# Causal attention: the sums of weights of three head pairs go through DRAM to 128 rows of 16, are inverted and gated there, and come back spread

## The chip, the cores and the metric

The kernel runs on one core of a Trainium2 chip. The metric is the device time of one execution in microseconds (us), as the median of several executions. Before the change it is 975.06 us, the median of 3 runs from 974.35 to 975.89 us. The profile shows one execution with a timestamp for every instruction.

## The reference, cut to what matters

One decoder layer in fp32 on an input of 2 sequences of 1024 tokens with 256 columns: a linear attention, a cross attention, and a feed-forward part that is a causal attention over gated experts. Only the third part is touched here:

```python
gates = sigmoid(x @ w_gate)                       # 8 heads x 8 experts for every token
sel   = argmax(gates, axis=-1)
gm    = one_hot(sel) * gates                      # the best expert's gate, zero for the others
values = einsum('bhne,ehdk,bnd->bhnk', gm, value_experts, x)
attn  = softmax(causal(q @ k.T))                  # 8 heads, 1024 x 1024
out   = einsum('bhij,bhjk->bhik', attn, values)
out   = einsum('bhne,ehkd,bhnk->bhnd', gm, output_experts, out).sum(axis=heads)
```

A row of the softmax is divided by its sum of weights, and the result is multiplied by the gate of the token before it goes to the output experts. Both factors are one number per head and token. The kernel puts them together: `oT * (1 / sum) * gate`.

## The kernel before, in words

The two sequences ("batches", b = 0 and 1) run one after the other through the same stages. The attention stage takes about 251 to 401 us in the first batch and about 725 to 875 us in the second. The sum over the output experts follows it.

**The attention stage.** The 8 heads are taken in order, two heads forming a pair: the even head has partitions 0 to 63, the odd one 64 to 127. Per head TensorE walks over 12 blocks (4 for the first 512 queries, 8 for the second 512; index n from 0 to 11). A block is a transposed score matmul (L1391, L1392, and a mask at L1394), an exponential on ScalarE (ACT, L749), and a matmul with the values (`weigh`, L1355), two blocks behind. The values carry 64 columns of ones for each pair, so the bank that collects the weighted values of a head on its 64 partitions collects the sum of weights on the other 64, the same sum on every one of them.

The exponentials need the maximum of each score row first. So while head h runs, TensorE also computes the plain scores of head h + 1 (`scores`, L1331), and VectorE (DVE) takes their maxima (`maximum`, L968) from three rotating PSUM banks: the fourth tile of a head can only be written when the first maximum has been taken. These 12 score tiles are spread over blocks 3 to 8 of head h (`SCORES_AT`); at block 9 the maxima are transposed and VectorE writes them as a row (`max_row`, L981), which the blocks of head h + 1 need. In even heads TensorE also makes the query and key projections of the next pair (`project`, L1315, after blocks 3, 5, 7 and 10).

**What VectorE does per head, in its order.** The loop `for h in range(1, H3)` runs `split(h)` (L954, L957: the key in two parts), the 12 maxima, and `max_row(h)`. Around `split(h)`, from h = 3 on, it normalises an earlier half of a pair: `PARTS[k]` is 512 columns of a pair (k = 0, 1 are pair 0; 2, 3 pair 1; 4, 5 pair 2; 6, 7, 8 pair 3, whose second half is cut in two). `inverted` (L989) is a reciprocal of `rden`, 128 partitions by 512 columns in two pieces of 256; `weighted` multiplies `rden` by the gates in `gb` (L997) and then `oT` by `rden` (L999). The parts k = 0 to 4 go into heads 3 to 7, and k = 5 comes behind the loop.

**Where the sums and gates come from.** ScalarE copies each finished bank (`evacuate`, L725 to L732): the sum rows into `rden` (64 x 512), the values into `oT`. `gate_rows` lies in DRAM; `spread_gates` (L716) sends the two gate rows of a pair over 64 partitions each into `gb`, on the DMA queue of ScalarE, at block 5 of each odd head.

**Behind the attention.** For the 32 (expert, pair) combinations in the order `SUMMED` (pair 3 comes first at n = 5), VectorE masks `oT` of the pair (L1043) and its rounding remainder (L1046), `masked(n)`, and TensorE adds 24 matmuls (L1418, L1424). The last three parts are normalised between them: `normalise(6)` after `masked(0)`, `normalise(7)` after `masked(1)`, `normalise(8)` after `masked(4)`. The output experts' pieces lie in two slots; the piece of expert 2 is fetched when TensorE has finished n = 5, the last use of expert 0.

**The order of the queues.** Every engine runs its instructions in program order, each behind its semaphore waits. SyncE (SP) issues almost all DMAs, also in order. In the first batch it loads 16 expert pieces, writes their two rounded halves back to DRAM (`halves_kept`, 512 KB each), and these loads and stores last until well into the attention; in the second batch the halves are read back and the attention stage has no such traffic. SP then fetches the masks (`fetch_mask`, L335).

## Time and profile before

| what | value |
|---|---|
| median of 3 runs | 975.06 us (974.35 to 975.89) |
| span of the profiled execution, first to last instruction | 972.8 us |
| median less that span (what lies around it) | 2.3 us |
| TensorE busy | 934.5 us (96%) |
| VectorE busy | 681.6 us (70%) |
| ScalarE busy | 387.8 us (40%) |
| GpSimd busy | 235.9 us (24%) |
| TensorE's granted clock, mean | 0.998 |

The page gives the span of the profiled execution, not a time of its own; the runs without a profile are 2.3 us above that span. Matmuls are pipelined, so that TensorE's busy time holds some waiting. The profile's "chain that ended last" goes back from the last instruction, at each step to what released it. "Idle before" in a row is the time for which the engine stood still just before that instruction, with what ended it.

### The profile page before, as it was taken

The numbers are of one execution on the slowest core, as the hardware profiler recorded it, in microseconds if no ns is written. First come the engines' busy times: TensorE is split into PE (matmuls) and PEld (weight loads), VectorE is DVE, ScalarE is ACT, GpSimd is POOL, SyncE is SP. The second block draws the span as 40 slices with busy tenths as digits, with TensorE's granted clock in tenths as the row PEclk, the third lists the DMA queues.
The fourth block names the chain that finished last, engine by engine and source line by source line (L and its number), as shares of the span: only waits on it lengthen the run. The fifth ranks groups of instructions, "written<-read, shape, count | busy, mean of one in ns | idle before, by whom it ended". The sixth has DMA issues, their size and how long they took to land.

```text
span 972.8 us, 14708 instructions
## 1 busy us (share of the span) xinstructions
PE 934.5 (96%) x5620; PEld 727.5 (75%) x5620; DVE 681.6 (70%) x1054; ACT 387.8 (40%) x672; POOL 235.9 (24%) x253
## 2 busy tenths in 40 slices
PE   6989999999999999999999998999999999999998
PEld 3668778887666655889976786888876656569998
DVE  4757566547557877888868666754674777879787
ACT  4535555030566766301033455720115655751000
POOL 6312322222533322136610042300041101411000
PEclk9999999999999999999999999999999999999999
DMA  7103000523255511256630000022220000123653
GB/s 257 49 18 114 2 1 5 162 101 130 65 155 193 198 40 44 65 173 175 179 124 1 1 2 1 1 94 87 86 84 4 23 23 0 30 70 109 184 180 124
DMA packets 33739, 81.56 MB, mean 84 GB/s; under 512 B 5847, under 2 KB 10551, under 8 KB 33671
## 3 DMA queue, kind: packets, MB, share of 16 engines
q1 hardware_dynamic: 32391, 76.44, 24.8%
q10 hardware_dynamic: 1280, 4.20, 1.6%
q8 instruction: 45, 0.74, 0.3%
q14 instruction: 23, 0.19, 0.1%
HBM read 61.26 MB, written 19.20 MB: 83 GB/s over the span
## 4 chain that ended last, share of the span: by engine, by line
PE 81%; DVE 10%; issue 3%; ACT 3%; DMA 2%; POOL 0%; ACTq 0%; SPq 0%; DVEq 0%; POOLq 0%
PE ps L1097 18%; PE ps L1418 10%; PE ps L1355 9%; PE ps L1424 5%; PE ps L1315 5%; PE ps L1270 5%; PE ps L1105 4%; PE ps L1331 4%; PE ps L1222 3%; DVE region L989 3%; PE ps L1284 3%; PE ps L1391 3%; PE ps L1392 2%; PE ps L1237 2%; PE ps L1139 2%
## 5 line engine op out<-in xcount | busy, mean ns | idle before, releaser
L1355 PE MATMUL ps<-region 128*128 128x512 f32 (+3 forms) x384 | 161.5, 504 | 0.0
L968 DVE TENSOR_REDUCE region<-ps 128x1 f32<-128x512 f32 (+1 forms) x192 | 98.2, 551 | 63.8 <-PE ps L1334 63.8
L749 ACT ACTIVATE region<-ps 128x512 f32<-128x512 f32 x192 | 92.2, 486 | 123.0 <-PE ps L1394 111.3
L1013 DVE COPY_PREDICATED region<-region,ps 128x512 f32<-128x512 uint32 x112 | 82.0, 736 | 72.0 <-PE ps L1097 71.3
L1418 PE MATMUL ps<-expert_hi,kst 128*128 128x256 f32 x512 | 125.1, 283 | 5.3 <-DMA expert_lo<-halves_kept 3.2
L1418 PE MATMUL ps<-expert_lo,kst 128*128 128x256 f32 x512 | 123.4, 280 | 0.0
L1097 PE MATMUL ps<-expert_hi,wide_hi 128*128 128x512 f32 x256 | 102.8, 401 | 0.0
L1418 PEld LDWEIGHTS ps<-expert_hi,kst 128*128 128x128 f32 x512 | 96.4, 188 | 6.6 <-DMA expert_lo<-halves_kept 3.6
L1097 PE MATMUL ps<-expert_hi,wide_lo 128*128 128x512 f32 x256 | 100.3, 392 | 0.0
L1097 PE MATMUL ps<-expert_lo,wide_hi 128*128 128x512 f32 x256 | 99.9, 390 | 0.0
L549 ACT ACTIVATE region<-ps 64x512 f32<-64x512 f32 (+4 forms) x146 | 80.8, 556 | 46.7 <-PE ps L1237 19.5
L1418 PEld LDWEIGHTS ps<-expert_lo,kst 128*128 128x128 f32 x512 | 96.5, 188 | 0.0
L1043 DVE TENSOR_TENSOR kst<-region 128x1024 fp32r<-128x1024 f32 x64 | 78.5, 1226 | 20.5 <-PE ps L1424 20.5
L421 POOL TENSOR_TENSOR qx<-region,qq 64x1024 fp32r<-64x1024 f32 x16 | 41.7, 2606 | 195.9 <-ACT qq L549 195.8
L1391 PE MATMUL ps<-qq,kst 128*128 128x512 f32 x192 | 86.9, 453 | 1.5 <-ACT region L749 1.3
L1331 PE MATMUL ps<-kst,qq 128*128 128x512 f32 (+1 forms) x192 | 79.7, 467 | 4.4 <-DVE region L968 4.4
L1424 PE MATMUL ps<-expert_hi,qq 128*128 128x256 f32 x512 | 72.5, 280 | 0.0
L1355 PEld LDWEIGHTS ps<-region 128*128 128x128 f32 x384 | 64.4, 194 | 6.2
L1392 PE MATMUL ps<-qx,kx 128*128 128x512 f32 x192 | 66.5, 346 | 0.0
L1424 PEld LDWEIGHTS ps<-expert_hi,qq 128*128 128x128 f32 x512 | 65.3, 188 | 0.0
L410 POOL TENSOR_TENSOR expert_lo<-expert,expert_hi 128x1024 fp32r<-128x1024 f32 x16 | 39.0, 2440 | 99.5 <-ACT expert_hi L549 99.5
L907 DVE TENSOR_REDUCE top<-ps 128x8 f32<-128x512 f32 (+1 forms) x64 | 34.2, 577 | 36.0 <-PE ps L1222 36.0
(148 smaller groups left out, 1772.3 us busy)
## 6 DMA issues: line engine op xcount, KB each, us to landing
region<-hot_rows SPq DMA_DIRECT2D x128, 128.0 KB, 3.4
expert_hi<-halves_kept SPq DMA_DIRECT2D x24, 512.0 KB, 3.6
expert_lo<-halves_kept SPq DMA_DIRECT2D x24, 512.0 KB, 5.0
halves_kept<-expert_hi SPq DMA_DIRECT2D x16, 512.0 KB, 5.1
halves_kept<-expert_lo SPq DMA_DIRECT2D x16, 512.0 KB, 5.9
expert<-in_value_experts SPq DMA_DIRECT2D x8, 512.0 KB, 4.2
expert<-in_output_experts SPq DMA_DIRECT2D x8, 512.0 KB, 4.3
gb<-gate_rows ACTq DMA_DIRECT2D x16, 256.0 KB, 3.8
```

The costliest lines, as they stand in the source:

```text
L549: act.activation(dst, src, ACT.Copy).then_inc(sem[name], 1)
L749: act.activation(PT[:, g % RING, lo:CH], ps[:, 4 + g % 2, 0:CH - lo], ACT.Exp).then_inc(sem["pt_ready"], 1)
L968: dve.tensor_reduce(mx[:, i, at_mx:at_mx + 1], ps[:, max_bank(h, m), 0:w], AX.X, ALU.max).then_inc(sem["s_max"], 1)
L1013: dve.copy_predicated(V3_heads[:, t], chosen.unsqueeze(3).broadcast_to([P, PAIRS3, 2, HD3]), ps[:, n % 4, :].rearrange("p (a i k) -> p a i ...
L1043: dve.tensor_tensor(kst[i][:, :], oT[:, p, :], masks[:, n % MASKS, :], ALU.mult).then_inc(sem["mo_hi_ready"], 1)
L1097: last = mm(ps[:, n % 4, :], x[:, i, rows_of], columns(w, i), start=(k == 0), stop=(k == len(parts) - 1))
L1331: last = mm(ps[:, max_bank(h, m), 0:w], qq[i][:, t * P:(t + 1) * P], kst[i][:, c * CH:c * CH + w], start=True, stop=not diagonal)
L1355: mm(ps[:, SUM_BANK[c], lo:CH], V3[:, j, h // 2, h % 2 * HD3:(h % 2 + 2) * HD3], PT[:, g % RING, lo:CH], start=(j == 0), stop=(j == TC * ( ...
L1391: mm(ps[:, bank, 0:w], kst[i][:, key], qq[i][:, query], start=True, stop=False)
L1392: last = mm(ps[:, bank, 0:w], kx[i][:, key], qx[i][:, query], start=False, stop=j < TC * c)
L1418: mm(ps[:, 4 + t // 2, t % 2 * D:(t % 2 + 1) * D], kst[n % 2][:, t * P:(t + 1) * P], w[:, slot, columns], start=(n == 0 and t % 2 == 0 and ...
L1424: return mm(ps[:, 4 + t // 2, t % 2 * D:(t % 2 + 1) * D], qq[n % 2][:, t * P:(t + 1) * P], expert_hi[:, slot, columns], start=False, stop= ...
```

## The change

For pairs 0 to 2, a sum is no longer inverted on 128 partitions by 1024 columns. ScalarE copies only one row of it per head (1 x 512, into row 32 * (h % 4) of `rden`); SP sends the row to DRAM (`den_rows`), and fetches the two rows of a pair as 128 rows of 16 (`den_cols`). VectorE inverts that 128 x 16 tile and multiplies it by the gates, which SP has fetched in the same layout (`gate_cols`). SP writes the result to DRAM (`factor_rows`), waits, and sends it over 64 partitions per head into `gb`. `weighted` then is one multiplication of `oT` by `gb`. The two tiles lie where the gate logits of the stage before were. Pair 3 keeps the old way. Its gates are spread by ScalarE after the last `evacuate` and no longer at block 5 of the last head; the other calls of `spread_gates` are gone. VectorE normalises the parts k = 0 to 3 in heads 4 to 7, and k = 4, 5 behind the loop.

```diff
+    BY_COLUMNS = PAIRS3 - 1
...
+        KN = 2 * S // P
...
+        hg_all = hg.rearrange("p t n -> p (t n)")
+        gate_cols = hg_all[:, 0:BY_COLUMNS * KN].rearrange("p (a k) -> p a k", a=BY_COLUMNS)
+        den_cols = hg_all[:, BY_COLUMNS * KN:(BY_COLUMNS + 2) * KN].rearrange("p (i k) -> p i k", i=2)
...
+        den_row = lambda h: P // 4 * (h % 4)
...
-        ROUND_AT = {(5, 4): 0, (5, 6): 1, (5, 8): 2, (5, 10): 3, (6, 6): 4, (7, 6): 5}
+        ROUND_AT = {(5, 4): 0, (5, 6): 1, (5, 8): 2, (6, 6): 3, (7, 9): 4, (7, 11): 5}
...
+            def columns_of(rows):
+                return rows.rearrange("h (q k) -> (h q) k", k=KN)
+            def keep_den(b, h):
+                until(sp, "o_sb", b, 2 * (h * NC + 1) + 1)
+                r = den_row(h)
+                sp.dma_start(den_rows[b, h:h + 1, :], rden[r:r + 1, :]).then_inc(den_kept, 16)
+            def turn_den(b, p):
+                n = b * BY_COLUMNS + p
+                sp.wait_ge(den_kept, 32 * (n + 1))
+                if n >= 2:
+                    sp.wait_ge(factors_kept, 16 * (n - 1))
+                sp.dma_start(den_cols[:, p % 2, :], columns_of(den_rows[b, 2 * p:2 * p + 2])).then_inc(den_in, 16)
+            def spread_factors(b, p):
+                n = b * BY_COLUMNS + p
+                until(sp, "factors_ready", b, p + 1)
+                sp.dma_start(columns_of(factor_rows[b, 2 * p:2 * p + 2]), den_cols[:, p % 2, :]
+                             ).then_inc(factors_kept, 16)
+                sp.wait_ge(factors_kept, 16 * (n + 1))
+                until(sp, "oT_ready", b, NC * p)
+                for i in range(2):
+                    sp.dma_start(gb[i * HALF:(i + 1) * HALF, :],
+                                 factor_rows[b, 2 * p + i:2 * p + i + 1, :].broadcast_to([HALF, S])
+                                 ).then_inc(gates_in, 16)
+            def turn_gates(b):
+                sp.wait_ge(rows_kept, 32 * (b + 1))
+                until(sp, "val_v", b, TT * (E3 - 1))
+                for p in range(BY_COLUMNS):
+                    sp.dma_start(gate_cols[:, p, :], columns_of(gate_rows[b, 2 * p:2 * p + 2])
+                                 ).then_inc(gate_cols_in, 16)
...
             for q in range(PIECES):
...
+                if q == E3:
+                    turn_gates(0)
+                if q == E3 + 4:
+                    keep_den(0, 0)
+                    keep_den(0, 1)
+                    turn_den(0, 0)
+                if q == E3 + 6:
+                    spread_factors(0, 0)
                 until(sp, "piece_lo", 0, q + 1)
...
-                sp.wait_ge(rows_kept, 32 * (b + 1))
+                if b:
+                    turn_gates(b)
+                for p in range(BY_COLUMNS):
+                    if b + p:
+                        keep_den(b, 2 * p)
+                        keep_den(b, 2 * p + 1)
+                        turn_den(b, p)
+                        spread_factors(b, p)
                 until(sp, "kst_ready", b, 2 * H3)
...
                     until(act, "av_used", b, h * NB + ENDS[c])
-                    if h % 2 == 0 and h:
-                        until(act, "oT_ready", b, (h // 2 - 1) * NC + c + 1)
-                    copy(rden[own:own + HALF, cs], ps[oth:oth + HALF, SUM_BANK[c], :], "o_sb")
+                    if h < 2 * BY_COLUMNS:
+                        r, n = den_row(h), 2 * BY_COLUMNS * b + h - 3
+                        if n > 0:
+                            act.wait_ge(den_kept, 16 * n)
+                        copy(rden[r:r + 1, cs], ps[oth:oth + 1, SUM_BANK[c], :], "o_sb")
+                    else:
+                        act.wait_ge(den_kept, 32 * BY_COLUMNS * (b + 1))
+                        copy(rden[own:own + HALF, cs], ps[oth:oth + HALF, SUM_BANK[c], :], "o_sb")
...
-                        if h % 2 and n == NB // 2 - 1:
-                            spread_gates(h // 2)
...
                 evacuate(H3 - 1, 1)
+                spread_gates()
                 for k in range(len(ROUND_AT), len(PARTS)):
                     rounded(k)
...
+                def factors(p):
+                    n = b * BY_COLUMNS + p
+                    if p == 0:
+                        dve.wait_ge(gate_cols_in, 16 * BY_COLUMNS * (b + 1))
+                    dve.wait_ge(den_in, 16 * (n + 1))
+                    step(dve.reciprocal(den_cols[:, p % 2, :], den_cols[:, p % 2, :]))
+                    dve.tensor_tensor(den_cols[:, p % 2, :], den_cols[:, p % 2, :], gate_cols[:, p, :], ALU.mult
+                                      ).then_inc(sem["factors_ready"], 1)
                 def weighted(k):
...
-                    step(dve.tensor_tensor(rden[:, cs], rden[:, cs], gb[:, cs], ALU.mult))
+                    if p >= BY_COLUMNS:
+                        step(dve.tensor_tensor(rden[:, cs], rden[:, cs], gb[:, cs], ALU.mult))
...
-                    dve.tensor_tensor(oT[:, p, cs], oT[:, p, cs], rden[:, cs], ALU.mult
+                    dve.tensor_tensor(oT[:, p, cs], oT[:, p, cs], (rden if p >= BY_COLUMNS else gb)[:, cs], ALU.mult
...
                 for h in range(1, H3):
-                    if h >= 3:
-                        _, c0, c1 = PARTS[h - 3]
-                        inverted(h - 3, c0, (c0 + c1) // 2)
                     split(h)
-                    if h >= 3:
-                        inverted(h - 3, (c0 + c1) // 2, c1)
-                        weighted(h - 3)
+                    if h >= 4:
+                        weighted(h - 4)
                     for m in range(NB):
                         maximum(h, m)
                     max_row(h)
-                normalise(H3 - 3)
+                    if h % 2 and h >= 3:
+                        factors((h - 3) // 2)
+                for k in range(H3 - 4, 2 * BY_COLUMNS):
+                    weighted(k)
```

## Rows read from the trace of the kernel before

**Rows 1.** The page: span; the chain that ended last, by engine.

```profile
span 972.8 us, 14708 instructions
...
PE 81%; DVE 10%; issue 3%; ACT 3%; DMA 2%; POOL 0%; ACTq 0%; SPq 0%; DVEq 0%; POOLq 0%
```

**Rows 2.** The whole chain in order of time (start us, us, what): the reciprocals in it.

```profile
314.28 1.76 DVE region L989
...
846.65 1.76 DVE region L989
```

**Rows 3.** VectorE's timeline, second batch (start us, us, engine, line, op, out<-in, count): `max_row` of heads 1 to 4.

```profile
744.04 1.21 DVE L981 SCALAR_TENSOR_TENSOR qx<-ps,const 8x1024 fp32r<-8x1024 f32 x1 [0.61 <-PE ps L1342]
...
762.25 1.22 DVE L981 SCALAR_TENSOR_TENSOR qx<-ps,const 8x1024 fp32r<-8x1024 f32 x1 [0.61 <-PE ps L1342]
...
782.80 1.21 DVE L981 SCALAR_TENSOR_TENSOR qx<-ps,const 8x1024 fp32r<-8x1024 f32 x1 [0.61 <-PE ps L1342]
...
801.96 1.22 DVE L981 SCALAR_TENSOR_TENSOR qx<-ps,const 8x1024 fp32r<-8x1024 f32 x1 [0.61 <-PE ps L1342]
```

**Rows 4.** TensorE's timeline: third and fourth score tile of heads 2, 4 and 7.

```profile
752.17 0.42 PE L1331 MATMUL ps<-kst,qq 128*128 128x384 f32 x1
753.26 0.58 PE L1331 MATMUL ps<-kst,qq 128*128 128x512 f32 x1
...
790.94 0.42 PE L1331 MATMUL ps<-kst,qq 128*128 128x384 f32 x1
793.00 0.49 PE L1331 MATMUL ps<-kst,qq 128*128 128x512 f32 x1 [0.63 <-DVE region L968]
...
373.68 0.42 PE L1331 MATMUL ps<-kst,qq 128*128 128x384 f32 x1
376.10 0.50 PE L1331 MATMUL ps<-kst,qq 128*128 128x512 f32 x1 [0.98 <-DVE region L968]
```

**Rows 5.** VectorE's timeline: the body of head 4, second and first batch.

```profile
792.67 3.07 DVE L968 TENSOR_REDUCE region<-ps 128x1 f32<-128x128 f32 x7
...
318.33 3.07 DVE L968 TENSOR_REDUCE region<-ps 128x1 f32<-128x128 f32 x7
```

**Rows 6.** Line L930: reciprocals of 128 x 16 and 128 x 8 (min/median/max in ns).

```profile
L930 DVE RECIPROCAL rc<-ps x32: 197/232/259, 72.8 to 620.3; 128x16 f32<-128x16 f32 x16, 128x8 f32<-128x8 f32 x16
```

**Rows 7.** DMA issues, 330.2 to 334 us: a store with nothing queued ahead (median us to landing).

```profile
halves_kept<-expert_hi SPq DMA_DIRECT2D x1, 512.0 KB, 2.6
```

**Rows 8.** Line L721: the gates' spread to 64 partitions, 16 DMAs.

```profile
DMA to landing us min/median/max: 3.4/3.8/4.7
```

**Rows 9.** SP's timeline and the DMA share by windows (last columns: clock, share, GB/s).

```profile
310.82 0.43 SPq L352 DMA_DIRECT2D halves_kept<-expert_lo  x1
...
314.00:316.00 2.00, 2.00 (x12) 1.29 (x11) 1.97 (x2) 1.98 (x3) 1.22 (x1) 1.00 0.98 399
316.00:318.00 2.00, 2.00 (x12) 1.28 (x10) 1.93 (x3) 1.98 (x5) 1.14 (x1) 1.00 0.05 16
```

**Rows 10.** ScalarE's timeline, last head: the gates' spread, the last evacuation.

```profile
392.47 0.45 ACTq L721 DMA_DIRECT2D gb<-gate_rows  x1
...
401.31 1.21 ACT L549 ACTIVATE region<-ps 64x512 f32<-64x512 f32 x2 [1.08 <-PE ps L1355]
```

**Rows 11.** VectorE's timeline behind the attention, first batch.

```profile
398.82 0.69 DVE L997 TENSOR_TENSOR region<-region,gb 128x512 f32<-128x512 f32 x1
...
415.33 1.23 DVE L1043 TENSOR_TENSOR kst<-region 128x1024 fp32r<-128x1024 f32 x1
```

**Rows 12.** TensorE's timeline, 402 to 430 us: all rows with idle time before them.

```profile
416.61 0.39 PE L1418 MATMUL ps<-expert_hi,kst 128*128 128x256 f32 x1 [1.05 <-DVE kst L1043]
426.72 0.39 PE L1418 MATMUL ps<-expert_hi,kst 128*128 128x256 f32 x1 [1.24 <-DMA expert_lo<-halves_kept]
```

**Rows 13.** The windows at the end of the span (busy PE, PEld, DVE, ACT, POOL; clock; share).

```profile
968.00:970.00 2.00, 1.27 (x11) 1.07 (x10) 1.98 (x3) 0.00 (x0) 0.00 (x0) 1.00 0.59 194
...
972.00:972.80 0.80, 0.00 (x0) 0.00 (x0) 0.00 (x0) 0.00 (x0) 0.00 (x0) 0.93 0.01 1
```

More of the change, by code:

```diff
@@ L177, in decoder_layer @@
         gate_rows = nc.dram_tensor("gate_rows", (B, H3, S), fp32, kind="Internal").ap()
+        den_rows = nc.dram_tensor("den_rows", (B, H3, S), fp32, kind="Internal").ap()
+        factor_rows = nc.dram_tensor("factor_rows", (B, H3, S), fp32, kind="Internal").ap()
         halves_kept = nc.dram_tensor("halves_kept", (2 * E3, 2, P, 4 * D), fp32, kind="Internal").ap()
@@ L197, in decoder_layer @@
             mo_hi_ready=NEP, mo_lo_ready=NEP,
-            x_lo=TT, windows_clear=1, piece_hi=2 * E3, piece_lo=2 * E3, mo_used=NEP, bank_full=TC - 1, out_ready=TC,
+            factors_ready=BY_COLUMNS, x_lo=TT, windows_clear=1, piece_hi=2 * E3, piece_lo=2 * E3, mo_used=NEP, bank_full=TC - 1, out_ready=TC,
         )
@@ L207, in decoder_layer @@
                 "c2k_ps", "c2v_ps", "c2k_sb", "c2v_sb", "dve_step"))
-        rows_kept, gates_in = (ctx.enter_context(nc.semaphore(n)) for n in ("rows_kept", "gates_in"))
+        rows_kept, gates_in, gate_cols_in, den_kept, den_in, factors_kept = (
+            ctx.enter_context(nc.semaphore(n)) for n in (
+                "rows_kept", "gates_in", "gate_cols_in", "den_kept", "den_in", "factors_kept"))
         x_in = [ctx.enter_context(nc.semaphore(f"x_in{i}")) for i in range(TT // 2)]
@@ L714, in rounded, with spread_gates @@
                     copy(o_lo(p)[:, c0:c1], oT[:, p, c0:c1], "o_round")
-                def spread_gates(p):
+                def spread_gates():
+                    p = PAIRS3 - 1
                     act.wait_ge(rows_kept, 32 * (b + 1))
```

## The prediction, made before the changed kernel was run

> **What bounds the kernel now.** I read the page first: in the chain of work that ended last TensorE has 81% of the span and VectorE 10% [rows 1]. So a microsecond taken from VectorE counts only where TensorE stands still for it. The chain in order of time then says where that may be: for pairs 0 to 2 it passes through twelve stretches of reciprocal (L989) and gate product (L997), six in each batch, 21.0 us together, the first and the last of them in [rows 2]. A chain says who released whom, not how long the other engine waited, so I measured the waiting in two more views.
>
> The first is the distance from one `max_row` to the next, a whole head of TensorE's work. From head 1 to head 2 of the second batch, where VectorE has nothing to invert, it is 762.25 - 744.04 = 18.21 us; from head 3 to head 4, with the same TensorE work and one inversion in VectorE's way, 801.96 - 782.80 = 19.16 us [rows 3]. The inversion, 5.2 us of VectorE, costs 0.95 us. The second is where TensorE pays: between the third and the fourth score tile of a head. Without inversion these are 1.09 us apart, with one 2.06 us, in the last head 2.42 us [rows 4]. So 0.97 us are to be had in heads 4 and 6, and 1.33 us in head 7. In heads 3 and 5 the stretch holds two more projections, and the chain goes through TensorE alone there: nothing to be had. All that the removed work costs is thus 2 x 0.97 + 1.33 = 3.3 us a batch, 6.5 us in all.
>
> Behind the attention it is the other way round. There TensorE waits for VectorE before n = 5 (1.05 us), and then for the expert piece that n = 5 frees (1.24 us) [rows 12]. VectorE works from 398.82 us, the gate product of part 6, to the mask of n = 5 at 415.33 us without a pause [rows 11]. Whatever makes that product late makes the whole rest of the batch late.
>
> **The change part by part.**
>
> *Pair 3's gates.* Before, ScalarE issued their spread at 392.47 us, and they were in before part 6 wanted them at 398.82 us [rows 10, 11]. Now the two DMAs stand behind the last `evacuate`, which can start at 401.31 us. The second is issued one issue (0.45 us) behind the first and lands 3.8 us later [rows 8, 10]: 401.31 + 0.45 + 3.8 = 405.56. `weighted(6)` waits for it on VectorE, and queued behind it are `masked(1)` and everything up to n = 5. So that whole row moves by 405.56 - 398.82 = 6.7 us, and n = 5 with it; its cover, the last six blocks of head 7, is gone. TensorE has only n = 0 to do meanwhile. Ends: with the fastest landing (3.4) it is 6.3 us; if the DMA goes only when the two copies of the evacuation (1.21 us) have ended, with the slowest landing (4.7), 8.9 us. I take 6.7, as ScalarE's queue issued at 392.47 us while its engine still had an exponential ahead of the DMA in program order to run. Twice: **+13.4 us** (12.6 to 17.8).
>
> *The round trip in heads 4 and 6.* `weighted(0)` and `weighted(2)` now come right behind `split`, and want factors which VectorE itself makes only at the end of the head before. Second batch, head 4: `max_row` of head 3 ends at 784.01. The small reciprocal is 0.23 us [rows 6], the product no more, with the handovers 0.55: 784.55. The store to DRAM is not in this trace; the nearest row is a store of 512 KB with a free queue, 2.6 us [rows 7], and I take that for 8 KB in 64-byte pieces: 787.15. Then two spreads, 0.5 and 3.8 us [rows 8]: 791.45. One product: the maxima start at 792.2, where before they started at 792.67 [rows 5]. Of the 0.97 us, 0.5 is gained. Ends: a store that costs nothing gains all 0.97; one of 3.4 us with a spread of 4.7 loses 1.2. The same holds for head 6 of both batches: three times, **-1.5 us** (-2.9 to +3.7).
>
> The Trainium skill ("DMA: Bandwidth & Descriptors", section "Anatomy of one DMA") gives a DMA a fixed cost of about 2.0 us, most of it the receipt of the write, and the bytes on top; by that this store is 2.0 us by estimate and the sum 1.4 us lower, and no row here shows so small a store.
>
> *The same in head 4 of the first batch.* There SP has just issued an expert load and two stores of 512 KB; the last at 310.82 [rows 9]. `spread_factors(0, 0)` stands behind them on the same queue. The DMA engines are busy until about 316 us (share 0.98 to 316, then 0.05) [rows 9]. I let the small store land at 317.0, the spreads at 321.3, the maxima start at 322.0; before it was 318.33 [rows 5]: **+3.7 us**. Ends: if the store passes the big ones, 0.2 gained; if it lands 1.5 us later still and the spread takes 4.7, 6 lost. Behind SP's waits stands `load_piece(15)`, but it waits for the rounding of piece 14 until 321 us anyway.
>
> *Head 7.* `weighted(3)` needs no new factors, so here all is gained: twice 1.3, **-2.6 us** (-2.7 to 0). `factors(2)` follows at 386 us; its factors are spread by 394 us, before masked(0) is needed at 401 us and before ScalarE's `rounded(4)` wants them at block 9 (398 us).
>
> *At nothing.* The evacuation copies one row instead of 64, along the same 512 columns: no change. `keep_den` and `turn_den` have most of a head's time (19 us) for two DMAs. `turn_gates` waits for products that are done at 251 us. The four issues of ScalarE's old spreads go, which may give back some tenths where they stood between exponentials; I put 0.6 us for both batches (0 to 2.9): **-0.6 us**.
>
> Sum: 13.4 - 1.5 + 3.7 - 2.6 - 0.6 = +12.4 us. The profiled span is 972.8 us [rows 1] and the median of the runs 2.3 us above it; with that unchanged, 972.8 + 12.4 + 2.3 = **987.5 us**.
>
> **The rivals.**
>
> *The clock falls in the new gap.* TensorE would stand from the end of n = 0 (about 404 us: it starts when the attention ends at 401 and an n takes 2.9 us, below) to the mask of n = 1 (two products and a mask behind the gates, 0.69 + 0.69 + 1.23 = 2.6 us [rows 11]; 408.2), some 4 us. At the end of the span it does nothing after 970 us, and the granted clock of the last 0.8 us is 0.93 on the mean instead of 1.00 [rows 13]: it begins to fall from 2.4 to 1.2 GHz. Against: the page's mean over the whole span is 0.998, so that no wait before has shown it. Price: TensorE did n = 0 to n = 4 from 401 us to 416.61 - 1.05 = 415.6 us [rows 12], 2.9 us each; at half speed an n takes 2.9 us more. VectorE takes some 15 us from the mask of n = 1 to that of n = 5, TensorE needs 4 x 2.9 = 11.6 for them: 3.6 us of slack. One slow n costs nothing, two cost 5.8 - 3.6 = 2.2 us a batch: up to 4.4 us more, 991.9 us. The Trainium skill ("TensorE: Matmul & The Clock Gate", Part 1) has the lower clock as the default that only activity lifts; by that rule the fall comes.
>
> *The round trips are slower than I think.* If 64-byte pieces cost 2 us more at each end, heads 4 and 6 lose 2 us instead of gaining 0.5, and the den rows come late too. For: no store of that form is in the trace. Price: 3 x 2.5 = 7.5: 995 us.
>
> *Faster: the chain is right.* If all 21.0 us of [rows 2] come off TensorE's path, the gain passes the 13.4 us behind the attention: 975.06 - 21.0 + 13.4 = 967.5 us. It decides once a batch gains more than 6.7 us before the last head's end. For: the chain as printed. Against: equal heads with and without the inversion differ by 0.95 us, not by 3.5 [rows 3].
>
> *The delay is swallowed.* If TensorE's waits behind n = 5 were for something not moved, a late n = 5 would cost nothing: 975 us less 1. Against: the piece awaited is fetched only when n = 5 is done.
>
> **How the numbers follow.** The forecast 0.74 (its own range 981 to 995), the clock 0.12, slow round trips 0.07, faster 0.04, swallowed 0.03. A measurement of this kernel tells about 0.2% (2 us) from no change; so slower 0.93, same 0.03, faster 0.04. The range: the low end takes the best ends of heads 4 and 6 with the fast landing and a store that passes the others, the high end slow round trips or slow clocks: 980 to 997 us.
>
> **What would show it.** In the trace after, VectorE's product with `gb` for part 6 waits some 7 us behind the attention for ScalarE's DMA, and TensorE has a gap of about 4 us before n = 1, in both batches. Between third and fourth score tile: about 1.6 us in head 4 of the second batch, 5 to 6 us in the first, 1.1 in head 7. There are no L989 rows of 256 columns before the last pair. The forecast is wrong if the spread of pair 3 is in by 400 us, or if equal heads with and without the inversion shrink by more than 1 us.

## The result, and the profile after

The changed kernel takes 993.09 us (median of 6 runs, 990.75 to 995.26), the kernel before on the same chip 975.47 us (6 runs, 974.35 to 981.29): a ratio of 1.0174 (95% interval 1.0148 to 1.0199). Slower, as forecast; 5.6 us above the predicted 987.5 us and inside the range. The profiled execution after took 993.52 us, with a span of 991.7 us, so 18.9 us more than the 972.8 us of [rows 1]. These 18.9 us are what the rest of this document accounts for.

The page of the kernel after: span, busy time, granted clock in 40 slices, the chain.

```profile
span 991.7 us, 14724 instructions
...
PE 941.4 (95%) x5620; PEld 733.5 (74%) x5620; DVE 633.4 (64%) x1032; ACT 388.4 (39%) x672; POOL 234.6 (24%) x253
...
PEclk9999999999999999999999899999999999998999
...
PE 85%; DVE 6%; DMA 4%; ACT 2%; issue 2%; POOL 1%; SPq 0%; ACTq 0%; POOLq 0%; DVEq 0%
```

VectorE has 48 us less to do than before (633.4 against 681.6 us), its share of the chain fell from 10% to 6%, and the kernel is slower. DMA's share doubled from 2% to 4%. That is the lesson of the case in one row: the work removed mostly ran beside TensorE, and what is waited for now are DMAs, above all the moved load of pair 3's gates, and in one head the round trip.

The distances between landmarks, as in [rows 3], from one `max_row` (L1050 after) to the next, and from the last one to the mask of n = 5, sum the difference up. Each is a difference of two start times in VectorE's timeline:

| stretch | before | after | difference | predicted |
|---|---|---|---|---|
| start of batch 0 (to its first `max_row`) | 242.91 | 241.83 | -1.08 | 0 |
| head 4, batch 0 | 18.97 | 24.79 | +5.82 | +3.7 |
| heads 4 and 6, the other three | 57.40 | 55.15 | -2.25 | -1.5 |
| head 7, both | 35.32 | 33.19 | -2.13 | -2.6 |
| other heads | 171.59 | 171.64 | +0.05 | -0.6 |
| last `max_row` to mask of n = 5, batch 0 | 30.33 | 37.97 | +7.64 | +6.7 |
| the same, batch 1 | 30.31 | 38.09 | +7.78 | +6.7 |
| mask of n = 5 to first `max_row` of batch 1 | 302.78 | 305.90 | +3.12 | 0 |
| the rest | 83.19 | 83.14 | -0.05 | 0 |

**Behind the attention.** VectorE's timeline of the kernel after, first batch; the number in brackets is the idle time before the row and what ended it. These rows answer to [rows 11].

```profile
395.48 1.29 DVE L1079 TENSOR_TENSOR region<-region,gb 128x512 f32<-128x512 f32 x2 [6.03 <-DMA gb<-factor_rows]
...
398.96 3.34 DVE L1058 RECIPROCAL region<-region 128x512 f32<-128x512 f32 x1
408.52 0.69 DVE L1077 TENSOR_TENSOR region<-region,gb 128x512 f32<-128x512 f32 x1 [6.22 <-DMA gb<-gate_rows]
...
409.86 1.22 DVE L1122 TENSOR_TENSOR kst<-region 128x1024 fp32r<-128x1024 f32 x1
411.00 2.29 DVE L1125 TENSOR_TENSOR qq<-wide_hi,region 128x1024 fp32r<-128x1024 f32 x1
...
425.84 1.22 DVE L1122 TENSOR_TENSOR kst<-region 128x1024 fp32r<-128x1024 f32 x1
```

The reciprocal is done at 402.30, and VectorE then waits 6.22 us for the gates, with everything up to n = 5 behind the waiting product. The issue of the gates in ScalarE's timeline, and GpSimd's (POOL) rounding remainder in its own:

```profile
403.82 0.59 ACT L613 ACTIVATE region<-ps 64x512 f32<-64x512 f32 x1 [0.56 <-PE ps L1434]
403.88 1.14 ACTq L786 DMA_DIRECT2D gb<-gate_rows  x2
```

```profile
410.75 1.46 POOL L589 TENSOR_TENSOR wide_lo<-region,wide_lo 128x512 fp32r<-128x512 f32 x1 [6.06 <-ACT wide_lo L613]
```

The queue issued the DMAs 0.06 us after the evacuation's first copy had started. From the last `max_row` the gate product is now 20.65 us away (408.52 - 387.87) where it was 13.82 (398.82 - 385.00): 6.83 us, predicted 6.7. The other 0.8 us are further down: the second product of `masked(1)` takes 2.29 us instead of 1.22, 1.07 us more, and 0.27 us come back at the next product with the gates (128 x 256), which took 0.69 us beside GpSimd and now takes 0.42. The same second product, and GpSimd's remainder for part 6, in the kernel before:

```profile
401.29 1.22 DVE L1046 TENSOR_TENSOR qq<-wide_hi,region 128x1024 fp32r<-128x1024 f32 x1
...
403.32 1.29 POOL L525 TENSOR_TENSOR wide_lo<-region,wide_lo 128x512 fp32r<-128x512 f32 x1 [7.12 <-ACT wide_lo L549]
```

There the remainder came behind `masked(1)`, beside the next reciprocal, because ScalarE still had the last evacuation ahead of it when the product was done. Now ScalarE has nothing else to do when the late product comes and rounds it at once, and the remainder falls on `masked(1)`.

What TensorE makes of it, in its own timeline (rows with idle time before them, and below them third and fourth score tiles, which answer to [rows 4]):

```profile
411.13 0.58 PE L1497 MATMUL ps<-expert_hi,kst 128*128 128x256 f32 x1 [4.38 <-DVE kst L1122]
417.06 0.38 PE L1497 MATMUL ps<-expert_hi,kst 128*128 128x256 f32 x1 [1.58 <-DVE kst L1122]
427.12 0.39 PE L1497 MATMUL ps<-expert_hi,kst 128*128 128x256 f32 x1 [1.32 <-DVE kst L1122]
...
893.86 0.58 PE L1497 MATMUL ps<-expert_hi,kst 128*128 128x256 f32 x1 [4.51 <-DVE kst L1122]
...
315.56 0.42 PE L1410 MATMUL ps<-kst,qq 128*128 128x384 f32 x1
321.90 0.80 PE L1410 MATMUL ps<-kst,qq 128*128 128x512 f32 x1 [4.91 <-DVE region L1037]
...
804.62 0.42 PE L1410 MATMUL ps<-kst,qq 128*128 128x384 f32 x1
805.97 0.49 PE L1410 MATMUL ps<-kst,qq 128*128 128x512 f32 x1
...
377.64 0.42 PE L1410 MATMUL ps<-kst,qq 128*128 128x384 f32 x1
378.73 0.58 PE L1410 MATMUL ps<-kst,qq 128*128 128x512 f32 x1
```

A gap of 4.38 us ahead of n = 1 in the first batch and 4.51 us in the second, where about 4 was forecast, and then the late n = 5 (at 427.12 us). Between third and fourth tile: 6.34 us in head 4 of the first batch (forecast 5 to 6), 1.35 us in that of the second (1.6), 1.09 us in head 7 (1.1).

**Head 4 of the first batch.** VectorE's timeline:

```profile
307.56 1.21 DVE L1050 SCALAR_TENSOR_TENSOR qx<-ps,const 8x1024 fp32r<-8x1024 f32 x1 [0.61 <-PE ps L1421]
308.69 0.23 DVE L1066 RECIPROCAL region<-region 128x16 f32<-128x16 f32 x1
...
320.95 0.69 DVE L1079 TENSOR_TENSOR region<-region,gb 128x512 f32<-128x512 f32 x1 [7.81 <-DMA gb<-factor_rows]
321.56 1.08 DVE L1037 TENSOR_REDUCE region<-ps 128x1 f32<-128x128 f32 x3
```

SP's timeline beside it:

```profile
308.91 0.33 SPq L390 DMA_DIRECT2D expert<-in_output_experts  x1
309.28 0.43 SPq L409 DMA_DIRECT2D halves_kept<-expert_hi  x1
309.76 0.43 SPq L409 DMA_DIRECT2D halves_kept<-expert_lo  x1
310.23 1.29 SPq L356 DMA_DIRECT2D factor_rows<-region  x1
316.16 1.14 SPq L361 DMA_DIRECT2D gb<-factor_rows  x2
```

The same store of 8 KB, in two DMA views (KB each, us from issue to landing): from 309 to 330 us, and for pair 1 from 354 to 362 us, with nothing ahead of it.

```profile
factor_rows<-region SPq DMA_DIRECT2D x1, 8.0 KB, 5.9
...
factor_rows<-region SPq DMA_DIRECT2D x1, 8.0 KB, 1.4
```

The store lands 1.4 us after its issue on a free queue and 5.9 us after it behind a load and two stores of 512 KB. The maxima start 14.00 us behind `max_row` (321.56 - 307.56) instead of 9.71: 4.29 us of the head's 5.82. The remaining 1.53 us are not in VectorE; the windows show them.

**The clock.** Windows of the kernel after: busy time (and count) of TensorE, weight loads, VectorE, ScalarE and GpSimd, then the granted clock, DMA share, GB/s.

```profile
322.00:324.00 2.00, 2.00 (x5) 1.42 (x6) 1.77 (x4) 0.00 (x0) 0.00 (x0) 0.50 0.89 305
...
412.00:414.00 2.00, 2.00 (x11) 2.00 (x11) 2.00 (x2) 0.00 (x0) 0.21 (x1) 0.50 0.00 0
...
558.00:560.00 2.00, 2.00 (x11) 2.00 (x11) 0.00 (x0) 0.34 (x1) 0.00 (x0) 0.50 0.00 0
```

In these stretches TensorE ran at 1.2 GHz (granted 0.50). Twice it had stood for over 4 us, in head 4 (4.91) and before n = 1 (4.38). The third time there was no such pause, and it concerns no edit; two windows of the kernel before, at the same place of the program in its first and second batch:

```profile
72.00:74.00 2.00, 2.00 (x10) 1.64 (x11) 0.68 (x2) 0.00 (x0) 0.00 (x0) 0.50 0.91 346
...
548.00:550.00 2.00, 2.00 (x18) 1.56 (x16) 0.68 (x2) 0.00 (x0) 0.00 (x0) 1.00 0.00 0
```

There, in the routing at the start of a batch, TensorE waits twice for VectorE, 0.97 and 0.8 us, in both kernels and both batches. The second of these waits in TensorE's timeline of the kernel before, first and second batch; the 16 matmuls behind it take 2.53 us in the one and 2.00 us in the other:

```profile
70.27 2.53 PE L1270 MATMUL ps<-region 128*128 128x102 f32 x16 [0.79 <-DVE region L922]
...
547.04 2.00 PE L1270 MATMUL ps<-region 128*128 128x102 f32 x16 [0.79 <-DVE region L922]
```

The clock fell behind these waits in the first batch of the profile before, in the second of the profile after, and not in the other two. To this the -1.08 and +3.12 us of the table are put down, 2.04 us that come with an execution and not with the change. For the +3.12 the kept profiles of all runs bear it out: from the mask of n = 5 to the first `max_row` of batch 1 it is 301.5 to 302.8 us in the seven where the clock stays at 1.00, and 303.3 to 305.9 us in the five where it falls somewhere in between. For the -1.08 they do so only in part: the start of batch 0 is 240.5 to 241.8 us without a fall and 241.7 to 242.9 us with one.

### The profile page after: what moved, and what is told of

It is laid out like the page before. It is cut to its first block, busy times and chain, and to the rows that moved or that the text cites. A ratio compares the mean times of both kernels' runs of the same rounds, so it can differ in the third digit from the quotient of the medians.

```text
span 991.7 us, 14724 instructions
## 1 busy us (share of the span) xinstructions
PE 941.4 (95%) x5620; PEld 733.5 (74%) x5620; DVE 633.4 (64%) x1032; ACT 388.4 (39%) x672; POOL 234.6 (24%) x253
## 4 chain that ended last, share of the span: by engine, by line
PE 85%; DVE 6%; DMA 4%; ACT 2%; issue 2%; POOL 1%; SPq 0%; ACTq 0%; POOLq 0%; DVEq 0%
PE ps L1176 18%; PE ps L1434 12%; PE ps L1497 9%; PE ps L1503 5%; PE ps L1349 5%; PE ps L1394 4%; PE ps L1184 4%; PE ps L1410 4%; PE ps L1470 3%; PE ps L1471 3%; PE ps L1301 3%; PE ps L1363 3%; PE ps L1316 2%; PE ps L1218 2%; PE ps L1255 2%
## 5 line engine op out<-in xcount | busy, mean ns | idle before, releaser
L1497 PE MATMUL ps<-expert_hi,kst 128*128 128x256 f32 x512 | 128.3, 288 | 17.0 <-DVE kst L1122 13.8
L1497 PE MATMUL ps<-expert_lo,kst 128*128 128x256 f32 x512 | 125.7, 283 | 0.0
L1497 PEld LDWEIGHTS ps<-expert_lo,kst 128*128 128x128 f32 x512 | 98.5, 192 | 0.0
L613 ACT ACTIVATE region<-ps 64x512 f32<-64x512 f32 (+5 forms) x146 | 80.8, 556 | 44.7 <-PE ps L1316 22.0
L485 POOL TENSOR_TENSOR qx<-region,qq 64x1024 fp32r<-64x1024 f32 x16 | 39.7, 2484 | 204.8 <-ACT qq L613 204.7
```

The source lines that it names most:

```text
L613: act.activation(dst, src, ACT.Copy).then_inc(sem[name], 1)
L1497: mm(ps[:, 4 + t // 2, t % 2 * D:(t % 2 + 1) * D], kst[n % 2][:, t * P:(t + 1) * P], w[:, slot, columns], start=(n == 0 and t % 2 == 0 and ...
```

## The experiments

**Pair 3's gates in a buffer of their own.** The spread goes back to block 5 of head 7; the gates go to a buffer that is free by then, under a semaphore of their own.

```diff
+        gb3 = xT[:, 0, :]
-                    until(act, "oT_ready", b, NC * p)
-                        act.dma_start(gb[i * HALF:(i + 1) * HALF, :],
+                        act.dma_start(gb3[i * HALF:(i + 1) * HALF, :],
+                        if h == H3 - 1 and n == NB // 2 - 1:
+                            spread_gates()
                 evacuate(H3 - 1, 1)
-                spread_gates()
```

> The changed kernel, but pair 3's gates get a buffer of their own (the free transposed input) and a semaphore of their own, so ScalarE spreads them at block 5 of the last head as the kernel before did. Theory A, the late spread costs the 7.64 us (first batch) and 7.78 us (second batch) by which the stretch from max_row of head 7 to n = 5 is longer: both stretches back to 31.6 us or less, the 4.4 us gap of TensorE before n = 1 gone, 993.1 - 15.4 = 977.7 us (974 to 981). Rival, the stretch is longer because the last weights arrive late or VectorE and GpSimd collide there: 988 us or more.

Measured: 982.83 us (10 runs, 978.60 to 985.17), ratio 1.0061 (1.0043 to 1.0079). So 10.3 us come back, not 15.4, and the time lies between the expectation and its rival. The gap before n = 1 is gone, but the mask of n = 5 stands 33.13 and 33.88 us behind the last `max_row`, still 2.8 and 3.6 us later than before. VectorE's timeline of this kernel shows what came next in line:

```profile
396.62 1.29 DVE L1083 TENSOR_TENSOR region<-region,gb 128x512 f32<-128x512 f32 x2 [6.26 <-DMA gb<-factor_rows]
...
403.48 0.69 DVE L1081 TENSOR_TENSOR region<-region,xT 128x512 f32<-128x512 f32 x1
...
404.81 2.32 DVE L1126 TENSOR_TENSOR kst<-region 128x1024 fp32r<-128x1024 f32 x1
407.06 2.31 DVE L1129 TENSOR_TENSOR qq<-wide_hi,region 128x1024 fp32r<-128x1024 f32 x1
```

and GpSimd's:

```profile
404.30 1.75 POOL L591 TENSOR_TENSOR wide_lo<-region,wide_lo 128x512 fp32r<-128x512 f32 x1 [0.89 <-ACT wide_lo L615]
406.72 1.56 POOL L591 TENSOR_TENSOR wide_lo<-region,wide_lo 128x512 fp32r<-128x512 f32 x1 [0.67 <-ACT wide_lo L615]
```

VectorE waits for pair 2's factors with `masked(0)` and the reciprocal of part 6 behind them: the gate product comes 14.71 us behind `max_row` (403.48 - 388.77) instead of 13.82. Then both products of `masked(1)` run at half pace beside GpSimd, 2.2 us more, so the rival was right that the two engines collide there. In the second batch the mask of n = 4 waits another 0.85 us for TensorE, whose clock has fallen behind a wait of 2.49 us (0.53 on the mean from 890 to 892 us). The Trainium skill ("SBUF — State Buffer", section "SBUF: two separate sides") has VectorE instructions with two SBUF inputs and GpSimd instructions share one pair of ports, which whoever starts first holds for its whole instruction. The rows agree: GpSimd's 404.30 ends at 406.05, and a full 1.22 us from there ends at 407.27; the product ended at 407.13 (404.81 + 2.32).

**The kernel before with the late spread alone.** `spread_gates(PAIRS3 - 1)` moves behind the last `evacuate`; nothing else is changed.

```diff
-                        if h % 2 and n == NB // 2 - 1:
+                        if h % 2 and n == NB // 2 - 1 and h < H3 - 1:
                             spread_gates(h // 2)
                 evacuate(H3 - 1, 1)
+                spread_gates(PAIRS3 - 1)
```

> The kernel before with one edit: pair 3's gates are spread after the last evacuation. No sums go through DRAM. Theory A: both batches lose 7 to 8 us behind the attention with nothing else changed, 975.5 + 15 = 990 us (987 to 994), and TensorE's clock falls in the gap. Rival, the delay comes from the sums' way through DRAM: no change, 975 us.

Measured: 992.47 us (4 runs, 990.09 to 994.06), ratio 1.0160 (1.0127 to 1.0193). From the last `max_row` to the mask of n = 5 it is 38.25 and 38.26 us, 7.9 us more than before; no head changed by over 0.1 us, and the clock fell in the gap as expected (0.50 from 408 to 410 us). One row tells it:

```profile
404.76 0.69 DVE L998 TENSOR_TENSOR region<-region,gb 128x512 f32<-128x512 f32 x1 [7.28 <-DMA gb<-gate_rows]
```

This one move makes the kernel before as slow as the whole change does. No sum goes through DRAM here, so the loss behind the attention is the late gates alone. That the two times are so close is partly chance: in the changed kernel head 4 of the first batch loses another 5.8 us, and the other even heads and head 7 give 4.4 us back.

**The product with the factors later in the head.** In the kernel after, `weighted(h - 4)` stands behind the sixth maximum of head h instead of ahead of the first.

```diff
-                    if h >= 4:
-                        weighted(h - 4)
                     for m in range(NB):
                         maximum(h, m)
+                        if h >= 4 and m == 5:
+                            weighted(h - 4)
```

> The changed kernel, but each head's product with the spread factors stands after the sixth of its twelve maxima instead of ahead of the first. Theory B, head 4 of the first batch loses 5.8 us because VectorE's wait for the spread stands ahead of the maxima: its max_row to max_row distance falls from 24.8 to 18.3 to 19 us, heads 4 and 6 elsewhere from 18.38 to about 18.2 us, 993.1 - 6.8 = 986.3 us (984 to 989). Rival, the stores and loads in flight slow the head itself, or the clock's fall has another cause: it stays above 23 us and the time at 992 us or more.

Measured: 986.77 us (4 runs, 986.13 to 987.12), ratio 1.0103 (1.0075 to 1.0131). Head 4 of the first batch is back at 18.92 us, heads 4 and 6 are at 18.23 to 18.24, which is the 18.21 us of a head without an inversion in [rows 3]. So the round trip through DRAM costs nothing if nobody waits for it.

**Both together.** The diffs of the first and the third experiment in one kernel.

> Both edits, own buffer for pair 3's gates and the product after the sixth maximum. If A and B are independent costs, 993.1 - 15.4 - 6.8 = 970.9 us (967 to 975), below the kernel before by what heads 4, 6 and 7 give back. Rival, the two hide behind one another: 975 us or more.

Measured: 976.47 us (10 runs, 974.53 to 979.76), ratio 1.0004 (0.9984 to 1.0024). The two effects add: 10.3 + 6.3 = 16.6 us off the 993.09. The expected 970.9 missed by 5.6 us, as the first experiment did by 5.1, for the same reasons: the tails are 33.06 and 34.09 us.

**The small store ahead of the large ones.** In SP's order `spread_factors(0, 0)` goes ahead of the expert load and the two stores.

```diff
-                if q == E3 + 6:
-                    spread_factors(0, 0)
                 until(sp, "piece_lo", 0, q + 1)
+                if q == E3 + 5:
+                    spread_factors(0, 0)
```

> The changed kernel; in the first batch SP sends the factors of pair 0 ahead of the expert load and the two 512 KB stores of that step instead of behind them. Theory B1, of the 5.8 us that head 4 loses there most is the small store's place in SP's queue (it landed 5.9 us after its issue, 1.4 us where the queue was free): the store lands in 1.4 us, head 4 takes 18.4 to 19.5 us instead of 24.8, time 987 to 988.5 us. Rival, the spread still shares the DMA engines with the stores and lands as late: 22 us or more for the head, 991 us or more.

Measured: 989.74 us (4 runs, 988.28 to 989.94), ratio 1.0122 (1.0107 to 1.0137). The store lands in 1.4 us, the product starts 8.16 us behind `max_row` (315.36 - 307.20) instead of 13.39. The head is 20.16 us, not under 19.5, and the time is above the expected 987 to 988.5 us: the expert load, now issued at 311.47 instead of 308.91, is late, and behind its rounding the exponential that TensorE waits for. ScalarE's timeline, then TensorE's:

```profile
317.33 1.06 ACT L613 ACTIVATE expert_hi<-expert 128x1024 fp32r<-128x1024 f32 x1 [1.12 <-DMA expert<-in_output_experts]
```

```profile
320.15 0.50 PE L1470 MATMUL ps<-qq,kst 128*128 128x512 f32 x1 [1.64 <-ACT region L819]
```

Where nothing delayed that load, with the product later in the head, TensorE's wait at this place was 0.57 us. That the order on SP's queue held the store is shown; that this turn of the order was not for nothing is shown too.

**Matmuls into the wait of head 4.** 60 extra bf16 matmuls of 128 columns, into a free bank, where TensorE waits for the first maximum of head 4 in the first batch.

```diff
+                    if b == 0 and h == 4 and m == MAX_BANKS:
+                        for _ in range(60):
+                            mm(ps[:, 6, 0:P], ident_b[:, :], neg[:, 0, :], start=True, stop=True)
```

> The changed kernel with 60 small extra matmuls (128 x 128, bf16, into an unused bank) where TensorE stands 4.9 us in head 4 of the first batch. The wait itself is left. Theory C, 1.5 of the 5.8 us is the lower clock behind that wait: the clock stays at 1.00 from 320 to 328 us, the head takes 23.3 us instead of 24.8, time 991.6 us. Rival, the 1.5 us is the catching up of VectorE and ScalarE: head 24.5 us or more, 993 us.

Measured: 990.42 us (4 runs, 987.85 to 991.75), ratio 1.0129 (1.0109 to 1.0149). The maxima still start 14.07 us behind `max_row`, the clock is 1.00 behind the wait, and the head takes 23.31 us instead of 24.79. So 1.5 us of that head's 5.8 were the clock.

**Masks first.** On top of both repairs: SP fetches the masks ahead of pair 2's factors, `masked(0)` stands ahead of `weighted(4)` and `weighted(5)`, and ScalarE's last two roundings come earlier.

```diff
-        ROUND_AT = {(5, 4): 0, (5, 6): 1, (5, 8): 2, (6, 6): 3, (7, 9): 4, (7, 11): 5}
+        ROUND_AT = {(5, 4): 0, (5, 6): 1, (5, 8): 2, (6, 6): 3, (7, 7): 4, (7, 8): 5}
                         turn_den(b, p)
+                        if p == BY_COLUMNS - 1:
...
+                            for n in range(MASKS):
+                                fetch_mask(b, n)
                         spread_factors(b, p)
...
-                for k in range(H3 - 4, 2 * BY_COLUMNS):
-                    weighted(k)
                     masked(n)
+                    if n == 0:
+                        for k in range(H3 - 4, 2 * BY_COLUMNS):
+                            weighted(k)
```

> Own buffer and later product as in the run with both edits; besides, SP fetches the first four masks before it waits for pair 2's factors, VectorE does masked(0) before the two products of pair 2, and ScalarE rounds those two parts at blocks 7 and 8 instead of 9 and 11. Theory D, the 2.8 us (first batch) and 3.8 us (second) by which the stretch behind max_row of head 7 is still longer than before (33.1 and 34.1 against 30.3 us to the mask of n = 5) are pair 2's late factors ahead of masked(0) (0.9 us) and GpSimd's late rounding remainders, which slow masked(1) from 1.2 to 2.3 us an operation: both stretches back to 30.3 to 31 us, 976.5 - 5.5 = 971 us (968.5 to 974). Rival, masked(1) is slow for another reason: 975 us or more.

Measured: 969.82 us (4 runs, 969.02 to 972.46), ratio 0.9930 (0.9909 to 0.9952). The tails are 30.48 and 30.44 us, within 0.2 us of the kernel before. VectorE's timeline: the mask no longer waits, and both products of `masked(1)` are at full pace again. The three moves were made in one run, so what each is worth alone is not shown. The collision has moved rather than gone: a remainder of GpSimd now lies beside the gate product of part 6, which takes 1.64 us instead of 0.69, but starts early enough for it.

```profile
383.23 1.23 DVE L1124 TENSOR_TENSOR kst<-region 128x1024 fp32r<-128x1024 f32 x1
...
397.26 1.22 DVE L1124 TENSOR_TENSOR kst<-region 128x1024 fp32r<-128x1024 f32 x1
398.40 1.22 DVE L1127 TENSOR_TENSOR qq<-wide_hi,region 128x1024 fp32r<-128x1024 f32 x1
```

**The clock at the batch starts, in three kernels.** 12 and 10 extra matmuls per batch where TensorE waits 0.97 and 0.8 us in the routing. In the kernel before, the kernel after, and the one with masks first:

```diff
                     if s == 2:
+                        pe.wait_ge(casts, 2)
+                        until(pe, "q_sb", b, 2 * NC)
+                        for _ in range(12):
+                            mm(ps[:, 7, 0:P], ident_b[:, :], neg[:, 0, :], start=True, stop=True)
                         until(pe, "n_blk", b, 2 * len(N1_RUNS))
                         if a + t == 0:
+                            for _ in range(10):
+                                mm(ps[:, 7, 0:P], ident_b[:, :], neg[:, 0, :], start=True, stop=True)
                             until(pe, "n_ready", b, len(N1_RUNS))
```

> The kernel before with 22 small extra matmuls per batch in the two short waits of TensorE at the start of each batch (where sums of the linear attention are placed). Nothing of the change is in it. Theory E, TensorE's clock falls behind these waits in some batches and not in others, whatever the kernel, and costs 1 to 3 us each time (3.1 us of the 18.9 us between the two profiles): the clock stays at 1.00 there in both batches and the time is 972 to 974.5 us. Rival, the fall does not hang on these waits: 975.5 us or more and the clock falls as before.

> The changed kernel with the 22 small extra matmuls per batch and nothing else. Theory E: the fall at 557 us goes (3.1 us in the profiled execution), those behind the waits for the late gates and in head 4 stay: 990 us (988.5 to 991.5), so the change alone costs 990 - 971.5 = 18.5 us when the luck of the clock at the batch's start is taken out of both. Rival, 992 us or more.

> The version with own buffer, later product and masks first, together with the 22 small extra matmuls per batch at the start of each batch. If the clock's falls there are independent of the rest (theory E), the falls at 70 and at 545 us go and the time is 969.8 - 3 = 966.5 us (965 to 968.5), below the kernel before with the extra matmuls alone (971.5) by the 5 us that heads 4, 6 and 7 give back. Rival, the fall only moves to another wait: 969 us or more.

Measured: before 971.52 us (4 runs, 970.74 to 973.55), ratio to itself without them 0.9942 (0.9924 to 0.9960); after 988.93 us (4 runs, 987.26 to 991.07), ratio 1.0128 (1.0098 to 1.0159); masks first 966.62 us (6 runs, 965.63 to 968.60), ratio 0.9902 (0.9881 to 0.9922). The first gained a little more than expected (972 to 974.5 us). The last beats both kernels, and it is 4.9 us below the kernel before with the same extra matmuls, about what heads 4, 6 and 7 give back. In the first and the last the clock is 1.00 up to the span's last 2.3 us; in the kernel after the falls behind its two long waits stay. Without the accident of the batch starts, the change costs 988.93 - 971.52 = 17.4 us; the two were run on different chips, and by the ratios, each to the kernel before on its own chip, it is 1.0128 / 0.9942 = 1.0187, some 18 us. The page of the last kernel, to be read beside the one above:

```profile
span 964.3 us, 14811 instructions
...
PEclk9999999999999999999999999999999999999999
...
PE 88%; DVE 5%; ACT 3%; issue 2%; DMA 2%; POOL 0%; SPq 0%; ACTq 0%; POOLq 0%; DVEq 0%
```

## Why the prediction was right

Its direction and its main term were right: the late gates were forecast at 6.7 us a batch and measured at 6.83, alone they make the kernel before 1.6% slower, and the small gains in the attention can't pay for them. That the range held the measured time is partly luck: its high end was set by slow round trips and by a clock that falls before n = 1, and what brought the time up was something else (below). Step by step:

- *Pair 3's gates.* +13.4 forecast, 7.64 + 7.78 = +15.4 measured. The wait itself was sized right, with its assumption that ScalarE's queue does not hold the DMAs back for the copies. What was missed is the row behind it: `masked(1)` takes 1.07 us longer beside GpSimd. "So that whole row moves by 6.7 us" took the durations in the row as fixed.
- *Heads 4 and 6.* -1.5 forecast, -2.25 measured. The store was taken from a row of 512 KB as 2.6 us; it is 1.4 us. The Trainium skill ("DMA: Bandwidth & Descriptors", section "Anatomy of one DMA") has a fixed cost of about 2.0 us for a DMA, nearer than 2.6 but still above the 1.4 of the trace; the section gives it for DMAs that GpSimd issues, a condition that the prediction left out, and this store is issued by SP.
- *Head 4 of the first batch.* +3.7 forecast, +5.82 measured: the mis-sized term of the sum. The store was to land 8.4 us behind the start of `max_row` and landed 8.6 us behind it (310.23 + 5.9 - 307.56); the spread took 4.8 instead of 4.3 us; the maxima started 4.29 us later than before. The other 1.5 us are the clock, which fell behind a wait of TensorE that the prediction had named (5 to 6 us between two tiles), without asking what it does to the clock.
- *Head 7.* -2.6 forecast, -2.13 measured. Its second half was a miss that the late gates hid: pair 2's factors were to be early enough, as `masked(0)` was needed only at 401 us. But on VectorE the reciprocal of part 6 stands behind that mask; it starts 11.09 us behind `max_row` instead of 10.43, and with the gates in a buffer of their own the delay is 0.89 us.
- *At nothing.* ScalarE's four issues were to give back 0.6 us; the other heads changed by +0.05 together. They stood where nobody waited. That a copy of one row takes as long as one of 64 is borne out: 588 against 593 ns on the mean, both of 512 columns.
- *The clock rival* had the mechanism and the wrong place. Its ground against itself, a mean clock of 0.998 "so that no wait before has shown it", was misread: the window from 72 to 74 us of that same trace stands at 0.50. The clock did fall in the gap before n = 1, for about 3 us in the first batch and 6 to 7 in the second (at 0.50 from 892 to 898 us). There it cost next to nothing: in the second batch n = 1 took 5.2 us (893.86 to 899.10) instead of 2.9, and TensorE still waited 0.68 us for the mask of n = 2; the tails of the two batches differ by 0.12 us. So its 991.9 us lies nearer the measured time than the forecast by chance. The Trainium skill ("TensorE: Matmul & The Clock Gate", Part 1) has the low clock as the default that activity lifts; the falls behind the waits of 4.91 and 4.38 us bear it out.
- *Faster* and *swallowed* are out: heads 4, 6 and 7 gave 4.4 us where nothing held the round trip up, not 21.0 (the chain's stretches are 14 with 23.0 us: two gate products of 0.99 us, at 374.14 and 848.44 us, were not counted), and the late n = 5 was paid in full in the kernel before with the late spread.

The gap between 12.4 forecast and 18.9 profiled is +2.0 for the gates, -0.75 for heads 4 and 6, +2.1 for the first head 4, +0.5 for head 7, +0.6 for ScalarE, and +2.0 for the clock at the batch starts, which is no part of the change.

What stays open: with the extra matmuls in the kernel before, head 5 of the first batch took 22.21 us in its profile instead of 20.63. The trace shows the way of the delay: the load of an expert piece landed 7.5 us after its issue instead of 5.9, ScalarE waited 3.20 us for it instead of 1.61, and TensorE stood 1.39 us for the exponential behind its rounding. Why that load was slower no run tells, nor why the clock falls at a batch start in one batch and not in the other.

## What to carry to other kernels

When a buffer's last user moves, follow its next writer: here one buffer for both kinds of factor pushed the gates' load behind the attention and cost more than the removed work had ever cost. Put a round trip through DRAM where its consumer comes last, not first, in the queue of the engine that waits, and look at what SP has queued ahead of a small store. After each repair look for the next late row: the gates, then the factors ahead of a mask and GpSimd beside a mask (both in one run) had to be taken away before the change was a gain.

## What the runs showed of the hardware

- The clock fell to 1.2 GHz behind waits of 0.97 and 0.8 us at a batch start, in one batch of an execution and not in the other, with the same instructions. Behind a wait of 1.9 to 2.5 us for an expert piece it fell too in three of the other kept profiles, and behind the same wait in the kernels before and after (2.00 and 1.96 us, second batch) it did not. Over 19 executions the kernel before took 972.69 to 979.50 us, at a mean granted clock of 0.999 for the shortest and 0.993 for the longest. 22 small matmuls a batch held the clock at the batch starts and took 0.6% off the time.
- A store of 8 KB to DRAM lands in 1.4 us, and in 5.9 us behind 1.5 MB on the same queue (the kernel after). In two other kept profiles one such store with nothing large ahead took 2.8 and 3.3 us.
- A VectorE product of 1.22 us (128 x 1024) takes 2.3 us when a GpSimd product of 1.5 to 1.8 us has started before it. A change in who is late moves such overlaps.
